# A phase-mixer layer with a ternary feed-forward: 16 token-sum blocks folded to 12 by an f16 add on VectorE

## The chip, the cores and the metric

The kernel runs on one core of one Trainium2 chip. The metric is device time in microseconds (us) of one execution; three runs of the kernel before gave 1516.4, 1513.59 and 1516.25 us, with a median of 1516.25 us.

## The reference

The input x has 16 sequences of 1024 tokens of 256 features. A first half normalises x over its features, and computes from it a phase and a memory:

```
omega = x @ W_omega.T + b_omega
phi   = cumsum(omega * exp(log_scale) / sqrt(position))          # over the sequence
cm_real, cm_imag   = x * cos(phi), x * sin(phi)
mem_real, mem_imag = cumsum(cm_real) / position, cumsum(cm_imag) / position
ret_real = mem_real * cos(phi) + mem_imag * sin(phi)
ret_imag = mem_imag * cos(phi) - mem_real * sin(phi)
context  = concat([cm_real, cm_imag, ret_real, ret_imag])         # 1024 features
h = gelu(layernorm(context) @ W1.T + b1) @ W2.T + b2              # 1024 -> 512 -> 256
x = x_input + x + h
```

The second half normalises again and adds `relu(x @ Wq1.T + b1) @ Wq2.T + b2`, 256 to 1024 to 256, with both weights rounded to -1, 0 or 1.

The layer norm of the context needs, for each token, the sum of its 1024 context features and the sum of their squares. The sum is what the change is about.

## The kernel before

The 16384 tokens are cut into 32 chunks of 512. Most tensors lie turned, with features on the 128 partitions and the 512 tokens of a chunk along the free dimension; so the 1024 context features are 8 blocks of 128x512 (`KC` = 8). Every f32 value that goes into a product is split into a high f16 half and a low f16 half (`ch` and `cl` for the context, made on ScalarE at line 645 and on VectorE at line 1382), and a product takes three passes: high by high, low by high, high by low.

The program is a pipeline written out by hand, one stream for each engine. Step s works on four chunks at once: `now` = s in the second half (the feed-forward), `nxt` = s+1 in the context's W1, gelu and W2, `ahead` = s+2 in phase, sums and retrieval, and `far` = s+3 in the first norm and omega. Steps run from -1 to 31. Within a step each engine's order is fixed by the program; engines meet by semaphores.

TensorE's order in a step is: `hidden` 0 and 1 (two of the four blocks of W1 on `nxt`, 24 matmuls each, line 989), `context_stats` (lines 959 and 965), `hidden` 2, `spread` (line 972, four transposes that spread the reciprocal deviation of each token over the partitions), `hidden` 3, then `ffn_in` 0 to 7 (line 1010) with `ffn_out` (line 1029) three blocks behind and `omega` (line 946) in between, `mixer_out` (W2, line 1060, 48 matmuls), and the last three `ffn_out`. `context_stats` gets the token sums by taking a 128x128 block of the context as the stationary operand and one column of ones as the moving one: for each of four token tiles, 16 such matmuls (8 blocks, high and low half) add into one PSUM column. Eight more do the same for the squares.

VectorE's order in a full step is: `fraction` (1300), `statistics_1` (1220 to 1230), `lean_2` (1236), `modulate_imag` (1313), `sums_imag` (a scan, 1321), `gains_1`, `modulate_real` (1307), `context_variance` (1387 to 1399, reads the token sums), `second_lo` (1442), `memory_imag`, `sums_real`, three `scale_hidden` (1406, which scale a finished `hidden` block and release its PSUM bank; `ffn_in` m waits for `scale_hidden` m), `first_rows_lo` (1264), `memory_real`, `retrieve_imag_cos`, the fourth `scale_hidden`, then the eight `relu_lo` (1450) among `gelu_lo` (1411), `context_lo` (1382) and others, `mixer_residual` (1418, waits for `mixer_out`), the phase scans (1287) and `statistics_2`.

GpSimd takes the power -1/2 three times (486, 510, 515), a product of 128x1024 into `qa` (563), additions of the squares (549, 556), and issues accumulating DMAs: `qa` is added into `rr` (491) and `qb` into `ri` (494). The sync engine's queue, in each step, waits for and issues four transposing loads of `turned2` (446), four of `turned1` (454), the load of the x rows four chunks on (458), and a store (461). In step -1 only some parts run; in step 0 VectorE also makes the signs of the second ternary weight (`signs(1)`, 1603 and 1604), and TensorE turns them.

In the last step `last_tiles` makes the output's last two blocks of products together, token tile by token tile, after VectorE's last `relu_lo`, and VectorE's `output` (1459) takes each half of the tiles as it is complete.

Of the kernel before, what the change touches and what calls it, by code (L numbers as in the profile page):

```python
# [17 lines left out]
ALU = mybir.AluOpType  # L18
# [25 lines left out]
def phase_mixer_layer(nc, x, w_omega, b_omega, log_scale, ln_gamma, ln_beta, w1, b1, w2, b2,  # L44
# [17 lines left out]
    with ctx:  # L62
# [98 lines left out]
        q_hi = sqr[:, 1, 0:CH // 2].bitcast(F16)  # L161
        q_lo = sqr[:, 1, CH // 2:CH].bitcast(F16)
        ones_h = sb("ones_h", [P, P], F16)
        turned2 = sb("turned2", [P, 2, KD, CH], F16)
        h2, l2 = turned2[:, 0], turned2[:, 1]
        rows1 = xs2[:, :, :].bitcast(F16).rearrange("p t (i d) -> p t i d", i=2)
# [123 lines left out]
        rl_done = sem("rl_done")  # L290
        f2_done = sem("f2_done")
        out_done = sem("out_done")
        tile_done = sem("tile_done")

        class Counts:

# [128 lines left out]
        def _(sp):  # L425
# [11 lines left out]
            sp.dma_start(pos_inv[:, :], pos_table[1].partition_broadcast(P)).then_inc(p_tab, 16)  # L437

            def step(s):
                if (c := s.chunk(0)) and c.index < CHUNKS - 1:  # L440
                    need(sp, h2_done, c)
                    need(sp, l2_done, c)
                    need_block(sp, f1_done, KF - 1, c, 1)
                    sp.sem_inc(turn2_begun, 1)
                    for j in range(NT):
                        sp.dma_start(turned2[:, :, :, j * P:(j + 1) * P].rearrange("p i k n -> p (i k) n"),
                                     rows2[:, j].rearrange("p i d -> p (i d)"), transpose=True).then_inc(turned2_done, 16)
                if (c := s.chunk(3)) and c.index >= 2:
                    need(sp, l1_done, c, 2)
                    need(sp, xf_done, c, 1)  # L450
                    need(sp, omega_done, c, 1)
                    sp.sem_inc(turn1_begun, 1)
                    for j in range(NT):
                        sp.dma_start(turned1[:, :, :, j * P:(j + 1) * P].rearrange("p i k n -> p (i k) n"),
                                     rows1[:, j].rearrange("p i d -> p (i d)"), transpose=True).then_inc(turned1_done, 16)
                if c := s.chunk(4):
                    need(sp, scaled_done, c, 2)
                    sp.dma_start(x_rows[:, c.b], x_v[c.index]).then_inc(x_loaded[c.b], 16)
                if (c := s.chunk(0)) and c.index < CHUNKS - 1:
                    need_dma(sp, x1_biased, c)  # L460
                    sp.dma_start(out_v[c.index], x1[:, c.b]).then_inc(stored[c.b], 16)
# [13 lines left out]
        def _(pool):  # L475
# [41 lines left out]
            def step(s):  # L517
                before, now, nxt, ahead, far = s.chunk(-1), s.chunk(0), s.chunk(1), s.chunk(2), s.chunk(3)
                if nxt and not now:
                    square_lo(nxt, ahead)  # L520
                if ahead:
                    base_bias(ahead)
                if now:
                    inverse_std_2(now)
                if before:
                    output_sum(before)
                if nxt and now:
                    square_lo(nxt, ahead)
                if far:
                    inverse_std_1(far)  # L530
                if now:
                    x1_bias(now)
                if nxt:
                    inverse_std_context(nxt)
                if ahead:
                    product_imag_sin(ahead)
                    retrieve(ahead)
                if ahead:
                    square_sums(ahead)
# [18 lines left out]
            def product_imag_sin(c):  # L558
                need(pool, mi_done, c)
                need(pool, sin_done, c)  # L560
                need(pool, sumr_done, c)
                need_sum(pool, rr_done, c, 1)
                pool.tensor_tensor(qa[:, :, :], mi[:, :, :], sn[:, :, :], ALU.mult).then_inc(qa_done, 1)  # L563

            first, second = first_chunks(pool)
# [359 lines left out]
        def _(pe):  # L925
# [24 lines left out]
            def context_stats(c, after):  # L950
# [2 lines left out]
                    need(pe, cl_done[part], c)  # L953
                if after:
                    need(pe, u_done, after)
                for j in range(NT):
                    halves = [(a, k) for k in range(KC) for a in (ch, cl)]
                    for i, (a, k) in enumerate(halves):
                        pe.matmul(ps[:, 3, j:j + 1], a[:, c.b, k, j * P:(j + 1) * P], ones_h[:, 0:1],  # L959
                                  start=(i == 0), stop=(i == len(halves) - 1))  # L960
                need(pe, qh_done, c)
                need(pe, ql_done, c)
# [68 lines left out]
                                     skip_group_check=True)  # L1031
                return last

            def last_tiles(c):

                for m in range(KF - 2, KF):
                    need_block(pe, rh_done, m, c)
                    need_block(pe, rl_done, m, c)
                for j in range(NT):
                    for m in range(KF - 2, KF):  # L1040
                        last = ffn_tile(m, j)
                    last.then_inc(tile_done, 1)

            def mixer_out(c, before):
                if before and c.index < CHUNKS - 1:
# [26 lines left out]
            def step(s):  # L1072
# [11 lines left out]
                if nxt:  # L1084
# [12 lines left out]
                    if not now:  # L1097
                        for n in SIGN_GROUPS[2:4]:
                            turn_signs(n)
                        mixer_out(nxt, now)  # L1100
                        omega(far)
                        return
                if now and not ahead:
                    for m in range(KF):
                        ffn_in(now, m, nxt)
                        if nxt and m == KE - 1:
                            mixer_out(nxt, now)
                        if m >= LAG:
                            ffn_out(now, m - LAG)
                    for m in range(KF - LAG, KF if nxt else KF - 2):  # L1110
                        ffn_out(now, m)
                        if nxt and m == KF - 3:
                            last_transposes(nxt)
                    if not nxt:
                        last_tiles(now)
                    return
                for m in range(KF):
                    if now:
# [7 lines left out]
                if now:  # L1126
                    for m in range(KF - LAG, KF):
                        ffn_out(now, m)

            def bank_free(n):  # L1130
                used = [i for i in range(n) if group_banks[i] == group_banks[n]]
# [71 lines left out]
        def _(dve):  # L1203
# [175 lines left out]
            def context_lo(c, part, src):  # L1379
# [2 lines left out]
                dve.tensor_tensor(cl[:, c.b, 2 * part:2 * part + 2], src, ch[:, c.b, 2 * part:2 * part + 2],  # L1382
                                  ALU.subtract).then_inc(cl_done[part], 1)

            def context_variance(c):
                need(dve, stats_done, c)
                dve.tensor_scalar(cmu[:, :], ps[:, 3, 0:NT], 1.0 / (RSTD_SCALE * C), None, ALU.mult).then_inc(cmu_done, 1)
# [65 lines left out]
            def output(c):  # L1453

                need_dma(dve, x1_biased, c)
                for half in range(2):
                    dve.wait_ge(tile_done, 2 * half + 2)
                    to = x1[:, c.b, 2 * half:2 * half + 2]
                    dve.scalar_tensor_tensor(out=to, in0=ps_rows_a[:, 2 * half:2 * half + 2], scalar=down[:, 4:5],
                                             in1=to, op0=ALU.mult, op1=ALU.add).then_inc(out_done, 1)  # L1460
# [1 line left out]
            def last_mixer(now, last):  # L1462

                lean_2(now)
                second_lo(now)
                context_variance(last)
                for m in range(KE):
                    scale_hidden(last, m)
# [13 lines left out]
            def step(s):  # L1482
# [15 lines left out]
                if nxt and not now:  # L1498
                    dve.wait_ge(p_fw1, 16)
                    signs(0, fw1_in, fw1_signs)  # L1500
                if now and now.index == 0:
                    dve.wait_ge(p_fw2, 16)
                    dve.wait_ge(p_tern, 2)
                    signs(1, fw2_in, fw2_signs)
                if ahead:
                    modulate_imag(ahead)
                    sums_imag(ahead)
                if far:
                    gains_1(far)
                if ahead:  # L1510
                    modulate_real(ahead)
                    carry_imag(ahead)
                if nxt:
                    context_variance(nxt)
                if now:
                    second_lo(now)
# [227 lines left out]
```

## Time and profile before

| | |
|---|---|
| median of three runs | 1516.25 us (1513.59 to 1516.4) |
| the profiled execution, its own time | 1516.13 us |
| its span, first to last instruction | 1514.3 us |
| mean granted TensorE clock | 0.991 |
| TensorE matmuls busy | 1465.8 us (97%) |
| VectorE busy | 1407.2 us (93%) |
| ScalarE busy | 1255.6 us (83%) |
| GpSimd busy | 558.7 us (37%) |

Busy time is the union of an engine's instructions. Two instructions of one engine overlap a little in it (the next starts before the last has drained), so what an instruction costs in a packed queue is the distance from its start to the next one's start. The span leaves 1.8 us of the profiled execution's time outside.

### The profile page before, as it was taken

To read this page: it belongs to the slowest core of one execution; us is meant where nothing else is said; L and a number is where in the kernel's file an instruction comes from. 1 tells how busy PE (TensorE), PEld (TensorE's weight loads), DVE (VectorE), ACT (ScalarE), POOL (GpSimd) and SP (SyncE) were. 2 spreads that over 40 slices of the span, in tenths; PEclk is the share of its full clock that TensorE was granted. 3 is DMA by queue.
4 is the path that set the end of the run, shared out by engine and by line. 5 is a ranking of instruction groups with operands and counts; after the bars stand their busy time and mean duration, and the time that the engine had idled before them with its cause. 6 is when DMAs were issued, how large, how long until landed. Compare 5 with 4: busy or idle time off the path is not lost.

```text
span 1514.3 us, 29961 instructions
## 1 busy us (share of the span) xinstructions
PE 1465.8 (97%) x10685; PEld 884.8 (58%) x10685; DVE 1407.2 (93%) x2325; ACT 1255.6 (83%) x1773; POOL 558.7 (37%) x393
## 2 busy tenths in 40 slices
PE   4789999999999999999999999999999999999998
PEld 2445566666566666555666655666655666665566
DVE  7989999999999999999999999999999999999844
ACT  6768888888888889888888888888888888888756
POOL 1223444333444433444433344443234443334321
PEclk9899999999999999999999999999999999999999
DMA  6436566656656666756666665666576566666542
GB/s 222 83 71 122 100 108 126 119 120 132 121 91 125 126 117 121 139 104 103 127 118 120 129 124 89 125 127 119 117 140 108 100 128 116 123 126 115 92 87 43
DMA packets 236035, 174.98 MB, mean 116 GB/s; under 512 B 139120, under 2 KB 222064, under 8 KB 235888
## 3 DMA queue, kind: packets, MB, share of 16 engines
q0 software_dynamic: 63984, 100.15, 40.5%
q1 hardware_dynamic: 170272, 69.25, 19.3%
q10 hardware_dynamic: 1632, 3.67, 0.7%
q8 instruction: 86, 1.41, 0.4%
q14 instruction: 61, 0.50, 0.1%
HBM read 24.13 MB, written 33.03 MB: 38 GB/s over the span
## 4 chain that ended last, share of the span: by engine, by line
PE 90%; DVE 4%; DMA 2%; issue 2%; ACT 2%; POOL 0%; ACTq 0%; DVEq 0%
PE ps L989 42%; PE ps L1029 14%; PE ps L1010 14%; PE ps L1060 11%; PE ps L946 5%; PE ps L959 3%; PE ps L972 1%; DMA arena<-in_L_attn_ln_beta 1%; DMA ri<-qb 1%; PE ps L965 0%; DVE mi L1321 0%; DMA rr<-qa 0%; DMA sqr<-turn 0%; ACT arena L716 0%; DVE bn L1220 0%
## 5 line engine op out<-in xcount | busy, mean ns | idle before, releaser
L989 PE MATMUL ps<-arena,w_hi 128*128 128x512 f16 x2048 | 610.3, 380 | 0.0
L989 PE MATMUL ps<-arena,w_lo 128*128 128x512 f16 x1024 | 388.7, 380 | 0.0
L989 PEld LDWEIGHTS ps<-arena,w_hi 128*128 128x128 f16 x2048 | 198.2, 98 | 221.3 <-issue 1.5
L1029 PE MATMUL ps<-fw_t,arena 128*128 128x256 f16 x2048 | 255.1, 273 | 3.0 <-DVE arena L1450 3.0
L1010 PE MATMUL ps<-turned,fw_t 128*128 128x512 f16 x1024 | 247.1, 379 | 0.4 <-issue 0.4
L1029 PEld LDWEIGHTS ps<-fw_t,arena 128*128 128x128 f16 x2048 | 199.9, 98 | 61.3 <-issue 13.7
L716 ACT ACTIVATE arena<-ps,relu_bias,relu_scale 128x512 f32<-128x512 f32 x256 | 196.8, 769 | 24.4 <-PE ps L1010 24.2
L1450 DVE TENSOR_TENSOR arena<-arena 128x512 f16<-128x512 f32 x256 | 173.1, 687 | 39.8 <-ACT arena L725 39.8
L1060 PE MATMUL ps<-w_hi,arena 128*128 128x256 f16 x1024 | 175.6, 275 | 4.8 <-DVE arena L1411 4.5
L989 PEld LDWEIGHTS ps<-arena,w_lo 128*128 128x128 f16 x1024 | 100.2, 98 | 121.3 <-issue 0.8
L725 ACT CAST arena<-arena 128x512 f16<-128x512 f32 x256 | 154.4, 614 | 4.3
L1010 PEld LDWEIGHTS ps<-turned,fw_t 128*128 128x128 f16 x1024 | 100.1, 98 | 93.7 <-issue 0.6
L1060 PE MATMUL ps<-w_lo,arena 128*128 128x256 f16 x512 | 140.9, 275 | 0.0
L491 POOL DMA_DIRECT2D rr<-qa x32 | 29.6, 925 | 226.1 <-DVE rr L1372 226.1
L549 POOL TENSOR_TENSOR sqr<-sqr 128x512 f32<-128x512 f32 x32 | 50.6, 1582 | 167.9 <-DVE arena L1382 153.8
L1060 PEld LDWEIGHTS ps<-w_hi,arena 128*128 128x128 f16 x1024 | 101.2, 99 | 17.9 <-issue 5.4
L563 POOL TENSOR_TENSOR qa<-mi,sn 128x1024 f32<-128x1024 f32 x31 | 73.2, 2361 | 86.4 <-DVE mr L1335 86.4
L613 ACT ACTIVATE xs<-x,lean,rs 128x256 f32<-128x256 f32 x128 | 66.4, 589 | 46.5 <-DVE lean L1236 46.5
L682 ACT ACTIVATE arena<-arena,b_full,z_down 128x512 f32<-128x512 f32 x128 | 96.9, 805 | 1.7 <-DVE arena L1406 1.3
L1406 DVE TENSOR_TENSOR arena<-ps,rb 128x512 f32<-128x512 f32 x128 | 82.1, 683 | 15.6 <-ACT rb L678 11.3
L1411 DVE SCALAR_TENSOR_TENSOR arena<-arena,up 128x512 f16<-128x512 f32 x128 | 95.0, 746 | 0.0
L546 POOL DMA_DIRECT2D sqr<-turn x32 | 27.4, 858 | 167.3 <-ACT turn L673 157.9
(189 smaller groups left out, 2805.2 us busy)
## 6 DMA issues: line engine op xcount, KB each, us to landing
x_rows<-in_L_attn_x SPq DMA_DIRECT2D x32, 512.0 KB, 4.6
rr<-qa POOLq DMA_DIRECT2D x32, 512.0 KB, 7.9
ri<-qb POOLq DMA_DIRECT2D x32, 512.0 KB, 8.5
sqr<-turn POOLq DMA_DIRECT2D x32, 512.0 KB, 5.5
base<-bias_rows POOLq DMA_DIRECT2D x32, 512.0 KB, 5.5
x<-bias_rows POOLq DMA_DIRECT2D x32, 512.0 KB, 5.9
out<-x SPq DMA_DIRECT2D x31, 512.0 KB, 5.7
out<-x POOLq DMA_DIRECT2D x31, 512.0 KB, 6.1
```

The lines of the kernel that those rows point to most:

```text
L563: pool.tensor_tensor(qa[:, :, :], mi[:, :, :], sn[:, :, :], ALU.mult).then_inc(qa_done, 1)
L682: act.activation(z[:, m], z[:, m], ACT.Gelu, scale=z_down[:, 0:1], bias=b1_full[:, m:m + 1])\
L716: act.activation(rf[:, m % SLOTS], ps[:, 4 + m % KE], ACT.Relu, scale=relu_scale[:, 0:1], bias=relu_bias[:, m:m + 1]).then_inc(relu_done, 1)
L725: act.copy(rh[:, m % SLOTS], rf[:, m % SLOTS]).then_inc(rh_done, 1)
L946: last = pe.matmul(ps[:, 2 + e], w[:, k, e * P:(e + 1) * P], a[:, k], start=(i == 0), stop=(i == len(passes) - 1))
L989: last = pe.matmul(ps[:, 4 + m], w[:, k, m * P:(m + 1) * P], a[:, c.b, k], start=(i == 0), stop=(i == len(passes) - 1))
L1010: last = pe.matmul(ps[:, 4 + m % KE], fw1_t[:, k, m * P:(m + 1) * P], a[:, k], start=(i == 0), stop=(i == len(passes) - 1))
L1029: last = pe.matmul(ps_rows_a[:, j], a[:, m % SLOTS, j * P:(j + 1) * P], fw2_t[:, m], start=(m == 0 and j % 2 == 0 and a is rh), stop=(m == ...
L1060: last = pe.matmul(rows[:, j], a[:, m, j * P:(j + 1) * P], w[:, m], start=(i == 0), stop=(i == len(passes) - 1))
L1406: dve.tensor_tensor(z[:, m], ps[:, 4 + m], rb[:, :], ALU.mult).then_inc(z_done[m], 1)
L1411: dve.scalar_tensor_tensor(out=gl[:, m], in0=z[:, m], scalar=up[:, 3:4], in1=gh[:, m], op0=ALU.mult, op1=ALU.subtract).then_inc(gl_done[m], 1)
L1450: dve.tensor_tensor(rl[:, m % SLOTS], rf[:, m % SLOTS], rh[:, m % SLOTS], ALU.subtract)\
```

## The change

VectorE gets a new instruction in each step, `fold_lo`: it adds the low halves of context blocks 4 to 7 to those of blocks 0 to 3, in f16, 128x2048 elements, into the buffer of `qa` (free at that time). TensorE's token sums then take the 8 high blocks and the 4 folded ones, 12 matmuls a token tile in place of 16, and wait for the fold; `qa`'s next writer on GpSimd waits for the sums. `fold_lo(nxt)` stands behind `modulate_imag(ahead)` in a normal step.

Besides: in step 0 `context_variance` stands ahead of `signs(1)`, and GpSimd's power for it ahead of a DMA issue; in step -1 TensorE does 12 products of 128x512 whose result nobody reads, ahead of `mixer_out`; the load of the x rows is first in the sync queue's step; and in the last step only the last block of products is held back, with the signal after each half of the tiles.

```diff
+        cl_fold = qa[:, :, :].rearrange("p k n -> p (k n)").bitcast(F16).rearrange("p (k n) -> p k n", k=KC // 2)
...
             def step(s):
+                if c := s.chunk(4):
+                    need(sp, scaled_done, c, 2)
+                    sp.dma_start(x_rows[:, c.b], x_v[c.index]).then_inc(x_loaded[c.b], 16)
                 if (c := s.chunk(0)) and c.index < CHUNKS - 1:
...
-                if c := s.chunk(4):
-                    need(sp, scaled_done, c, 2)
-                    sp.dma_start(x_rows[:, c.b], x_v[c.index]).then_inc(x_loaded[c.b], 16)
...
+                if nxt and now and now.index == 0:
+                    inverse_std_context(nxt)
                 if now:
                     x1_bias(now)
-                if nxt:
+                if nxt and not (now and now.index == 0):
                     inverse_std_context(nxt)
...
                 need_sum(pool, rr_done, c, 1)
+                need(pool, stats_done, c, 1)
                 pool.tensor_tensor(qa[:, :, :], mi[:, :, :], sn[:, :, :], ALU.mult).then_inc(qa_done, 1)
...
+                need(pe, clf_done, c)
                 for j in range(NT):
-                    halves = [(a, k) for k in range(KC) for a in (ch, cl)]
-                    for i, (a, k) in enumerate(halves):
-                        pe.matmul(ps[:, 3, j:j + 1], a[:, c.b, k, j * P:(j + 1) * P], ones_h[:, 0:1],
+                    halves = [ch[:, c.b, k] for k in range(KC)] + [cl_fold[:, k] for k in range(KC // 2)]
+                    for i, a in enumerate(halves):
+                        pe.matmul(ps[:, 3, j:j + 1], a[:, j * P:(j + 1) * P], ones_h[:, 0:1],
                                   start=(i == 0), stop=(i == len(halves) - 1))
...
-            def last_tiles(c):
-
-                for m in range(KF - 2, KF):
-                    need_block(pe, rh_done, m, c)
-                    need_block(pe, rl_done, m, c)
+            def last_unit(c):
+
+                need_block(pe, rh_done, KF - 1, c)
+                need_block(pe, rl_done, KF - 1, c)
                 for j in range(NT):
-                    for m in range(KF - 2, KF):
-                        last = ffn_tile(m, j)
-                    last.then_inc(tile_done, 1)
+                    last = ffn_tile(KF - 1, j)
+                    if j % 2:
+                        last.then_inc(pair_done, 1)
...
+                        need(pe, z_done[2], nxt)
+                        idle_products()
                         mixer_out(nxt, now)
...
+            def idle_products():
+
+                for i in range(12):
+                    pe.matmul(ps[:, 6], wo_hi[:, 0, 0:P], w1_hi[:, i % KC], start=True, stop=True)
...
+            def fold_lo(c):
+                need(dve, cl_done[3], c)
+                need_sum(dve, rr_done, c)
+                dve.tensor_tensor(cl_fold, cl[:, c.b, 0:KC // 2], cl[:, c.b, KC // 2:KC], ALU.add).then_inc(clf_done, 1)
...
+                if ahead:
+                    modulate_imag(ahead)
+                if nxt:
+                    fold_lo(nxt)
                 if now and now.index == 0:
+                    context_variance(nxt)
                     dve.wait_ge(p_fw2, 16)
                     dve.wait_ge(p_tern, 2)
                     signs(1, fw2_in, fw2_signs)
                 if ahead:
-                    modulate_imag(ahead)
                     sums_imag(ahead)
...
-                if nxt:
+                if nxt and not (now and now.index == 0):
                     context_variance(nxt)
```

## Rows read from the trace of the kernel before

**Rows 1.** The page: busy time, share of the span and instructions of the engines.

```profile
PE 1465.8 (97%) x10685; PEld 884.8 (58%) x10685; DVE 1407.2 (93%) x2325; ACT 1255.6 (83%) x1773; POOL 558.7 (37%) x393
```

**Rows 2.** The chain of waits in one middle step: start, us, what.

```profile
703.38 1.58 PE ps L959 x64
...
715.97 3.45 PE ps L1010 x16
...
735.08 2.62 PE ps L1029 x24
```

**Rows 3.** Busy times in that step; VectorE's largest wait over 16 steps.

```profile
693.01:737.70 44.69, 44.69 (x330) 26.91 (x328) 43.14 (x70) 38.38 (x55) 17.59 (x12) 1.00 0.63 119
...
DVE arena L1450 <- ACT arena L725: 12.7, 16, 0.9
```

**Rows 4.** Timeline of VectorE, then GpSimd, same step: start, us busy, instruction, [idle before].

```profile
699.03 1.58 DVE L1230 TENSOR_SCALAR ve<-mv 128x4 f32<-128x4 f32 x1
...
701.85 2.46 DVE L1321 TENSOR_TENSOR_SCAN mi<-ones,mi_carry,cmi 128x512 f32<-128x512 f32 x2
...
711.50 1.89 DVE L1406 TENSOR_TENSOR arena<-ps,rb 128x512 f32<-128x512 f32 x3 [0.30 <-ACT rb L678]
713.31 1.32 DVE L1264 TENSOR_TENSOR xs<-qb,xs 128x1024 f16<-128x1024 f32 x1
...
716.82 0.68 DVE L1406 TENSOR_TENSOR arena<-ps,rb 128x512 f32<-128x512 f32 x1
718.33 0.69 DVE L1450 TENSOR_TENSOR arena<-arena 128x512 f16<-128x512 f32 x1 [0.84 <-ACT arena L725]
...
734.47 0.68 DVE L1450 TENSOR_TENSOR arena<-arena 128x512 f16<-128x512 f32 x1
735.11 1.28 DVE L1418 SCALAR_TENSOR_TENSOR x<-ps,h_down,base 128x1024 f32<-128x1024 f32 x1
...
746.76 2.34 DVE L1321 TENSOR_TENSOR_SCAN mi<-ones,cmi 128x512 f32<-128x512 f32 x2
...
711.18 2.36 POOL L563 TENSOR_TENSOR qa<-mi,sn 128x1024 f32<-128x1024 f32 x1 [2.83 <-DVE mr L1335]
```

**Rows 5.** Groups of VectorE instructions nearest to the fold: count, busy us, mean ns.

```profile
L1313 DVE TENSOR_TENSOR cmi<-xf,sn 128x1024 f32<-128x1024 f32 x32 | 38.8, 1212 | 0.0
...
L1450 DVE TENSOR_TENSOR arena<-arena 128x512 f16<-128x512 f32 x256 | 173.1, 687 | 39.8 <-ACT arena L725 39.8
...
L1604 DVE TENSOR_SCALAR arena<-arena,neg_thr 128x2048 f16<-128x2048 f32 x1 | 1.3, 1275 | 0.0
```

**Rows 6.** Timelines, chain and one stretch of steps -1 and 0.

```profile
71.84 1.74 PE L959 MATMUL ps<-ones_h,arena 128*128 128x1 f16 x64
...
73.17 1.21 DVE L1313 TENSOR_TENSOR cmi<-xf,sn 128x1024 f32<-128x1024 f32 x1
...
82.55 1.88 DVE L1406 TENSOR_TENSOR arena<-ps,rb 128x512 f32<-128x512 f32 x3
...
91.43 0.58 SPq L458 DMA_DIRECT2D x_rows<-in_L_attn_x  x1
...
91.76 10.00 DMA ri<-qb
...
95.00:100.00 5.00, 5.00 (x27) 3.62 (x25) 3.48 (x3) 1.05 (x1) 0.00 (x0) 0.53 0.95 222
...
114.97 1.74 PE L959 MATMUL ps<-ones_h,arena 128*128 128x1 f16 x64
...
115.88 1.27 DVE L1603 TENSOR_SCALAR arena<-arena,thr 128x2048 f16<-128x2048 f32 x1
...
128.75 1.89 DVE L1406 TENSOR_TENSOR arena<-ps,rb 128x512 f32<-128x512 f32 x3
```

**Rows 7.** The chain of waits at the very end.

```profile
1508.78 0.14 issue
1508.91 1.92 PE ps L1029 x16
```

More of the change, by code:

```diff
@@ L292, in phase_mixer_layer @@
         out_done = sem("out_done")
-        tile_done = sem("tile_done")
+        pair_done = sem("pair_done")
+        clf_done = sem("clf_done")
         class Counts:
@@ L1109, in step @@
                             ffn_out(now, m - LAG)
-                    for m in range(KF - LAG, KF if nxt else KF - 2):
+                    for m in range(KF - LAG, KF if nxt else KF - 1):
                         ffn_out(now, m)
@@ L1114, in step @@
                     if not nxt:
-                        last_tiles(now)
+                        last_unit(now)
                     return
@@ L1456, in output @@
                 for half in range(2):
-                    dve.wait_ge(tile_done, 2 * half + 2)
+                    dve.wait_ge(pair_done, half + 1)
                     to = x1[:, c.b, 2 * half:2 * half + 2]
@@ L1465, in last_mixer @@
                 second_lo(now)
+                fold_lo(last)
                 context_variance(last)
```

## The prediction

> **What bounds the kernel now.** I read the page first. TensorE is busy for 97% of the span and VectorE for 93% [rows 1]. The chain of waits then shows that from about 140 to 1431 us it never leaves TensorE: every step has the same pieces, three of which stand in [rows 2], and no wait lies between them. The busy times by stretch give a step of 44.69 us with TensorE busy for all of it and VectorE for 43.14 [rows 3]; other steps give 44.67 to 44.69. So TensorE sets the step, with VectorE close behind. How close is the question, for the change takes work from the first and gives work to the second.
>
> VectorE's slack is read from its timeline [rows 4], between starts. Two of the 1406 instructions lie 0.60 apart ((1.89 - 0.68) / 2). The fourth starts at 716.82, so `relu_lo` 0 could start at 717.42; it starts at 718.33, behind ScalarE, which is itself behind TensorE's first `ffn_in`. That is 0.91 us of slack; over 16 steps the same wait is 12.7 us [rows 3], 0.79 a step as listed and 0.87 with the 0.07 by which packed instructions overlap. `mixer_residual` at 735.11 follows the `relu_lo` of 734.47 by 0.64, 0.04 over the packed distance: the end of `mixer_out` at 735.08 [rows 2] just holds it. The third wait, 0.30 us at 711.50, gives nothing back: the instruction behind those three, line 1264, takes 1.32 and only gets going when GpSimd's product ends at 711.18 + 2.36 = 713.54. An earlier start would only lengthen it. So a packed VectorE step is 44.68 - 0.87 - 0.04 = **43.77 us**. The small gaps between dependent tiny instructions stay.
>
> **What TensorE gives up.** 64 matmuls of one column take 1.58 us [rows 2], 24.7 ns each; 16 fewer give 0.39 us. Its own step becomes 44.29 us. If nothing else mattered, 28 such steps would gain 11 us.
>
> **What the fold costs.** No row shows a `tensor_tensor` with both inputs and output in f16. Its inputs are 2048 halves a partition, as many bytes as the 1024 f32 of line 1313, which takes 1.21 [rows 5] and, as 128x1024 instructions do, 1.14 from start to start. Line 1604 shows that VectorE can pass 2048 elements in 1.275 us, two for each it passes in the f32 instructions. If the fold went one element at a time, lines 1450 and 1313 extrapolate to 1212 + 2 x (1212 - 687) = 2262 ns, some 2.2 from start to start. Nothing points under 1.14. I take 1.14, the row with equal operation and equal bytes, and keep 2.2 as the far end.
>
> The Trainium skill ("VectorE: DVE Perf Modes", the perf-mode tier table) says that `tensor_tensor` on 16-bit data in SBUF runs at two elements a cycle, 1224 ns for 2048, and at one a cycle in fp32, 2293 ns. By the first the sum below stays as it is, by the second it is the third rival's. The table is about bf16, and no row here shows the f16 case.
>
> **The new step.** VectorE packed: 43.77 + 1.14 = 44.91 us, over TensorE's 44.29 and over the 44.68 of before. VectorE becomes the bound, and TensorE waits for it. Where it waits decides whether more is lost. Count from S, the start of `sums_imag` (701.85), right behind the fold. The fold ends at S + 0.08, and VectorE to TensorE takes 0.14 [rows 7], so the token sums start at S + 0.22 in place of S + 1.36 (703.21 on the timeline). With 0.39 less to do there, the first `ffn_in` comes 1.53 earlier relative to VectorE: at S + 12.43 (715.81 before; the chain sets the piece 0.16 later). `ffn_in` 3, 2.59 later, wants to go at S + 15.02. But it needs `scale_hidden` 3, which starts at S + 14.97 and ends at S + 15.65; with the hop it is free at S + 15.79. So TensorE stops there for 0.77 us. From there to the end of `mixer_out` TensorE needs what it needed before, 735.08 - 718.40 = 16.68, and ends at S + 32.47. VectorE would reach `mixer_residual`, packed, at 735.11 - 701.85 - 0.91 - 0.04 = S + 32.31, and starts at S + 32.50. That is 0.19 us more in each step, from a loop that runs fold, `scale_hidden` 3, `ffn_in`, `mixer_out`, `mixer_residual`. Then the rest of VectorE's step and the next fold follow unbroken. The step becomes 44.91 + 0.19 = **45.10 us, 0.42 more than before**. From step 0 to step 28, the last full one, that is 28 x 0.42 = **+11.8 us**; without the loop 28 x 0.23 = 6.4.
>
> Nothing else comes up in time by this count. `relu_lo` 0 needs 2.52 from the first `ffn_in`, S + 14.95, and VectorE is there at S + 15.57. GpSimd's power for the variance hangs on VectorE and is done 0.3 before `spread` asks. GpSimd's new wait for the sums ends at about S + 1.6, and its product starts at S + 9.3. The x rows are asked for 25 us sooner and leave the time in which `rr` and `ri` are added; nothing on the bound waits for those in a middle step, so this is worth nothing there. In the middle it could only matter by delaying the bias DMAs that it now meets, and those have most of a step.
>
> **The start.** In step -1 TensorE's sums stand at 71.84, but the fold comes behind line 1313 of 73.17 and ends near 75.5 [rows 6]. TensorE stops 3.8 us, `spread` comes some 3 us late, and line 1406 with it moves from 82.55 to about 85.2: +2.65 where the fold alone would be +1.14. That moves the issue of the `ri` addition from 91.76 to 94.4. It took 10.00 us, with the x rows issued at 91.43 in between; without them I take 8, so it lands at +0.6 (between -0.5 and +2.6). The 12 products fill about 2.6 us of TensorE's wait ahead of `mixer_out`, which before ran with the granted clock at 0.53 from 95 to 100 us, most of it at the lower level of 1.2 GHz. At the full clock that stretch would be 5.00 x 0.47 = 2.4 us shorter; that pays for the later start of `mixer_out` and no more. In step 0 the fold ends near 118.9 (115.88 + 0.6 + 1.14 + 1.22). TensorE's sums (114.97 before) wait 4 us for it, and then VectorE, with `context_variance` next in its queue, waits 1.6 for the sums. The four-odd instructions of the variance come sooner, but they only served a `spread` that isn't on VectorE's bound. VectorE reaches line 1406 near 132.1 in place of 128.75 and `relu_lo` 0 near 138.3. In the steady rhythm of before, counted back from 718.33 by 13 steps, it stood at 137.5. So the start costs **+0.8 to +1.0 us**, between -1 and +3.
>
> **The end.** In steps 29 and 30 VectorE has no `far` chunk and much idle time; the fold is hidden and TensorE gains 2 x 0.39. In the last step 8 of the 16 matmuls in the 1.92 us piece [rows 7] move ahead of VectorE's last `relu_lo`; VectorE's two 0.75 us instructions then follow one another, and 0.6 is gained. Together **-1.4 us**, with 0.1 given back where step 28 leaves TensorE.
>
> **Sum.** +11.8 + 1.0 - 1.3 = +11.5 on 1516.13 us of the profiled execution, whose time is 0.1 from the median: **1527.5 us**.
>
> **Rivals.** (1) VectorE bounds, but the loop through `scale_hidden` 3 doesn't close: 6.4 + 1.0 - 1.3, 1522 us. For it speaks that 0.19 hangs on a hop of 0.14 and two distances; against it that all of these are read from one regular step. With a good start 1519.5. (2) The other side: the fold finds room and TensorE stays the bound at 44.29: -11.0 + 1.0 - 1.3, 1505 us. That needs 0.62 us of VectorE's packed 44.91 to go. The one place is line 1230, a 128x4 instruction that takes 1.58 us [rows 4] and shares its time with one of GpSimd's additions; other 128x4 instructions of VectorE take 0.2. It decides if GpSimd's chain ends 0.62 us sooner relative to VectorE. Against it: that chain starts from VectorE's own line 1436, and nothing moves between them. (3) The fold runs one element at a time: 1.06 more in 28 steps and twice at the start, 1559 us.
>
> **Chances.** Forecast (1523 to 1531) 0.48; rival 1 (1517 to 1523) 0.27, of which a third falls below 1519.3; rival 2 0.13; rival 3 0.07; the rest, mixtures near no change, 0.05. The range that holds 8 in 10 leaves out rivals 2 and 3: 1516 to 1531. A measurement of this kernel tells 0.2%, 3 us, from no change. Faster 0.13, same 0.15, slower 0.72.
>
> **What would show it.** The step of the chain near 45.1 us; the fold at 1.2 us; no idle time before `relu_lo` 0 on VectorE; TensorE idle before line 1010 behind line 1406 (0.6 to 0.8 a step) and a little before line 959; 48 matmuls in 1.19. I am wrong if the step is 44.3 (then line 1230 is short), or if the fold takes over 2 us.

## The result

The changed kernel takes 1526.76 us (median of four runs, 1525.65 to 1527.73) against 1516.24 us before: a ratio of 1.0073 with a 95% interval of 1.006 to 1.0085. It is slower, as forecast, and 0.7 us from the forecast of 1527.5. Its profiled execution took 1527.73 us with a span of 1525.8, which is 11.5 above the span of before. The sum comes out right, but not all of its terms do. How they divide is the main subject below.

The page, the same line as [rows 1]. TensorE has lost 4.8 us of busy time and VectorE has gained 37.6. Below it stands the chain of waits by engine, in which VectorE now leads.

```profile
PE 1461.0 (96%) x10185; PEld 868.5 (57%) x10185; DVE 1444.8 (95%) x2357; ACT 1256.8 (82%) x1773; POOL 560.1 (37%) x393
...
DVE 40%; PE 33%; issue 13%; ACT 7%; DMA 3%; SPq 2%; DVEq 1%; POOL 0%; ACTq 0%
```

The groups by line, VectorE: the fold and the instructions around it (count, busy us, mean ns, idle before). Line numbers of after are some 5 to 17 higher: 1242 is the old 1230, 1276 the old 1264, 1423 is `scale_hidden`, 1435 `mixer_residual`, 1467 `relu_lo`, 951 `omega`, 965 the token sums, 995 `hidden`, 1016 `ffn_in`, 1035 `ffn_out`, 1065 `mixer_out`.

```profile
L1276 DVE TENSOR_TENSOR xs<-qb,xs 128x1024 f16<-128x1024 f32 x30 | 47.3, 1577 | 0.0
L1242 DVE TENSOR_SCALAR ve<-mv 128x4 f32<-128x4 f32 x32 | 44.8, 1401 | 1.2 <-DVE mv L1237 0.2
L1325 DVE TENSOR_TENSOR cmi<-xf,sn 128x1024 f32<-128x1024 f32 x32 | 40.8, 1275 | 0.1
L1400 DVE TENSOR_TENSOR qa<-arena 128x2048 f16<-128x2048 f16 x32 | 38.7, 1211 | 0.0
```

The busy times by stretch, one middle step, from one `mixer_residual` to the next; it answers to [rows 3]. TensorE now has gaps, and what VectorE lacks to the full stretch is some 0.5 us of small gaps between dependent tiny instructions.

```profile
743.95:788.82 44.87, 44.52 (x314) 26.35 (x313) 44.33 (x75) 38.26 (x54) 17.69 (x13) 1.00 0.63 118
```

The timeline of VectorE in that step: start, us busy, instruction. It answers to [rows 4].

```profile
743.30 0.68 DVE L1467 TENSOR_TENSOR arena<-arena 128x512 f16<-128x512 f32 x1
743.95 1.28 DVE L1435 SCALAR_TENSOR_TENSOR x<-ps,h_down,base 128x1024 f32<-128x1024 f32 x1
...
752.75 1.57 DVE L1242 TENSOR_SCALAR ve<-mv 128x4 f32<-128x4 f32 x1
...
754.30 1.21 DVE L1325 TENSOR_TENSOR cmi<-xf,sn 128x1024 f32<-128x1024 f32 x1
755.44 1.21 DVE L1400 TENSOR_TENSOR qa<-arena 128x2048 f16<-128x2048 f16 x1
756.58 2.33 DVE L1333 TENSOR_TENSOR_SCAN mi<-ones,cmi 128x512 f32<-128x512 f32 x2
...
771.36 0.68 DVE L1423 TENSOR_TENSOR arena<-ps,rb 128x512 f32<-128x512 f32 x1
771.96 0.68 DVE L1467 TENSOR_TENSOR arena<-arena 128x512 f16<-128x512 f32 x1
...
788.08 0.68 DVE L1467 TENSOR_TENSOR arena<-arena 128x512 f16<-128x512 f32 x1
788.82 1.28 DVE L1435 SCALAR_TENSOR_TENSOR x<-ps,h_down,base 128x1024 f32<-128x1024 f32 x1
```

The fold lies 1.14 from start to start, `relu_lo` 0 follows `scale_hidden` 3 at the packed distance of 0.60 with no idle time, and the last `relu_lo` stands 0.74 ahead of `mixer_residual` where 0.60 would be packed: 0.14 us of waiting for `mixer_out`. This step and the one of [rows 4] are not quite alike: every second step's scans carry on from the chunk before.

What TensorE waits for between 140 and 1420 us (total, times, longest):

```profile
PE ps L1016 <- DVE arena L1423: 8.3, 22, 0.6
PE ps L1016 <- DMA turned<-rows: 3.4, 5, 1.3
PE ps L951 <- DMA turned<-xs: 2.5, 1, 2.5
```

The first row is the stop that was forecast, `ffn_in` behind `scale_hidden` 3, seen 22 times, 0.4 us each as listed. The other two were not forecast: transposing loads that land late. The chain of waits of the same step shows the forecast loop closed, and its next piece behind the 5.25 us of `mixer_out` is VectorE again, by way of `mixer_residual`:

```profile
772.09 1.04 PE ps L1016 x4
...
783.54 5.25 PE ps L1065 x48
...
790.02 2.45 DVE ph L1299 x2
```

To see where the 11.5 us lie, take the start of `mixer_residual` in each step from VectorE's timeline (before: 154.50 in step 0 and 1405.31 in step 28; after: 157.16 and 1417.92). Up to step 0 the changed kernel loses 2.7 us, over the 28 steps 1260.76 - 1250.81 = 9.95, and from there to the end of the span it gains 1.1. Of the 28 steps most last 44.82 to 44.89, on average 44.85; a step of before lasts 44.68. So 28 x 0.17 = 4.8 us come from the regular step. Another 5.0 lie in a few long steps: 47.50, 45.77, 45.42 and smaller ones. The last 0.2 is the first of the 28, which before took only 44.46.

### The profile page after: what moved, and what is told of

Its sections match the earlier page's. It is cut to its first block, busy times and chain, and to the rows that moved or that the text cites. A ratio compares the mean times of both kernels' runs of the same rounds, so it can differ in the third digit from the quotient of the medians.

```text
span 1525.8 us, 29056 instructions
## 1 busy us (share of the span) xinstructions
PE 1461.0 (96%) x10185; PEld 868.5 (57%) x10185; DVE 1444.8 (95%) x2357; ACT 1256.8 (82%) x1773; POOL 560.1 (37%) x393
## 4 chain that ended last, share of the span: by engine, by line
DVE 40%; PE 33%; issue 13%; ACT 7%; DMA 3%; SPq 2%; DVEq 1%; POOL 0%; ACTq 0%
PE ps L1065 9%; PE ps L1016 8%; PE ps L1035 8%; DVE ph L1299 4%; PE ps L951 4%; DVE mr L1347 4%; ACT xs L618 3%; DVE arena L1423 3%; PE ps L995 3%; DVE bn L1232 3%; DVE mi L1333 3%; DVE bn L1442 3%; DVE xs L1276 2%; DVE cmr L1319 2%; DVE mi L1368 2%
## 5 line engine op out<-in xcount | busy, mean ns | idle before, releaser
L1016 PE MATMUL ps<-turned,fw_t 128*128 128x512 f16 x1024 | 251.3, 379 | 13.9 <-DVE arena L1423 8.3
L517 POOL TENSOR_TENSOR crs<-cve,minus_half 128x4 f32<-128x4 f32 x32 | 61.5, 1923 | 99.2 <-DVE cve L1416 99.2
```

The source lines that it names most:

```text
L1016: last = pe.matmul(ps[:, 4 + m % KE], fw1_t[:, k, m * P:(m + 1) * P], a[:, k], start=(i == 0), stop=(i == len(passes) - 1))
```

## The experiments

Theory A is the prediction's: VectorE is the bound, by the fold's time and a loop of 0.19. Rival B: the fold finds room in the stall of the old line 1230 and TensorE stays the bound. Times stand with the run of the kernel before on the same chip. "Step" is the regular distance between two `mixer_residual`, "start" its place in step 0. Unless said otherwise an edit is against the changed kernel.

### The fold and the sums without the other edits

The x loads, the order of step 0, the idle products and the last step are as before; the fold stands behind `modulate_imag`.

> The kernel before with the fold alone (fold, 12-block sums and their waits), none of the edits to the first steps, the last step and the order of the x load. Theory A (the time goes up because VectorE, packed, is longer than TensorE's step): a middle step near 44.9 us as in the changed kernel, so about 28 x 0.25 to 0.35 over before, plus some 4 us in steps -1 and 0, where nothing pays for the later sums: 1527 to 1530 us. Theory B (the other edits are what costs): close to 1505 us, 28 x 0.39 under before.

Measured 1535.95 us (1532.08 to 1539.16), ratio 1.0129 [1.0113, 1.0145]. The regular step is that of after, 44.84 to 44.87; the start is at 159.54. The four executions differ by 7 us. That is 6 us above the range expected of theory A, which held no long steps: 1266.37 - 28 x 44.85 = 10.6 us lie in them, where the changed kernel had 5.0. The regular steps account for 5, and the start for another 5. B is out.

### The other edits without the fold

```diff
-                need(pe, clf_done, c)
...
-                    halves = [ch[:, c.b, k] for k in range(KC)] + [cl_fold[:, k] for k in range(KC // 2)]
+                    halves = [(a, k) for k in range(KC) for a in (ch, cl)]
...
-                if nxt:
-                    fold_lo(nxt)
```

> The changed kernel without the fold: 16-block sums, all the other edits kept. Theory A: a middle step of 44.68 us as before, and some us less at the two ends: 1508 to 1514 us. Theory B: 1520 us or more.

Measured 1511.85 us (1511.27 to 1512.54), ratio 0.9971 [0.996, 0.9983]. They gain 3.4 us at the start (151.15 against 154.50) and 0.3 at the end; the step stays at 44.68. So the fold with its sums costs about 15 us in the changed kernel, and the rest gives back 4 of it.

### The fold ahead of the statistics

The stall of the old line 1230 is tested with the fold's place alone: ahead of `statistics_1(far)`, in place of behind `modulate_imag`.

```diff
+                if nxt:
+                    fold_lo(nxt)
                 if far:
                     statistics_1(far)
...
                 if ahead:
                     modulate_imag(ahead)
-                if nxt:
-                    fold_lo(nxt)
```

> The changed kernel with the fold moved ahead of the first-norm statistics of the far chunk in VectorE's order. There the 128x4 instruction that takes 1.56 us, because it meets GpSimd's addition, comes 1.14 us later and should meet only its last 0.4 us. Theory A1 (that stall ends with GpSimd's addition, whatever VectorE does before it): the fold fills the stall, VectorE packed comes to 43.8 us or less, TensorE is the bound again at 44.29 us, and the time is 1504 to 1508 us. Rival A2 (the stall has a length of its own and follows the instruction): the step stays near 44.9 us, the time at 1524 to 1527 us.

Measured 1505.35 us (1503.89 to 1505.8), ratio 0.9927 [0.9914, 0.9939]: the same instructions in another order are 21 us faster. Its timeline of VectorE, then of GpSimd:

```profile
738.42 1.22 DVE L1400 TENSOR_TENSOR qa<-arena 128x2048 f16<-128x2048 f16 x1
739.56 1.40 DVE L1232 BATCH_NORM_STATS2 bn<-x_rows 128x6 f32<-128x256 f32 x4
...
741.48 0.43 DVE L1242 TENSOR_SCALAR ve<-mv 128x4 f32<-128x4 f32 x1
...
740.22 1.66 POOL L560 TENSOR_TENSOR sqr<-sqr 128x512 f16<-128x512 f32 x1
```

And GpSimd in the changed kernel, beside line 1242 at 752.75 above:

```profile
752.62 1.66 POOL L560 TENSOR_TENSOR sqr<-sqr 128x512 f16<-128x512 f32 x1
```

GpSimd's addition ends at 754.28 in the one and at 741.88 in the other. Line 1242 ends at 754.32 and 741.91. So it ends when the addition does in both places, and most of its 1.57 us are a wait. The wait shrinks by 1.14, exactly the fold that now runs in it. GpSimd's chain hangs on a VectorE instruction ahead of the fold (line 1453), so the fold doesn't push it back: the addition starts 3.0 us after that instruction in both kernels. VectorE's step falls under TensorE's, and the step is 44.27 to 44.29 in 26 of 28 cases.

The Trainium skill ("SBUF — State Buffer", the section on SBUF's two separate sides) says that VectorE and GpSimd share one pair of ports, and that of a GpSimd instruction and a VectorE instruction that needs the pair (one in a mode that reads through two ports, or one with two inputs in SBUF) whichever starts first holds it for the whole instruction. The trace agrees in this place: GpSimd's addition starts first, 752.62 against 752.75 and 740.22 against 741.48, and both ends are 0.03 to 0.04 apart.

### Half the fold

Two blocks are folded, and 14 are summed.

```diff
-...+ [cl_fold[:, k] for k in range(KC // 2)]
+...+ [cl[:, c.b, k] for k in range(4)] + [cl_fold[:, k] for k in range(2)]
...
-dve.tensor_tensor(cl_fold, cl[:, c.b, 0:KC // 2], cl[:, c.b, KC // 2:KC], ALU.add)
+dve.tensor_tensor(cl_fold[:, 0:2], cl[:, c.b, 4:6], cl[:, c.b, 6:8], ALU.add)
```

> The changed kernel with half the fold: two low blocks are added to two others (128x1024 in f16), TensorE sums 14 blocks. Theory A: VectorE packed 44.85 - 0.53 = 44.32 us, TensorE 44.68 - 0.20 = 44.48 us and the bound again: 28 x 0.55 under the changed kernel, 1510 to 1513 us. Rival (TensorE loses its time by the wait for the fold as such, or by late transposing loads, and not by VectorE's length): a step between 44.7 and 45.0 us, 1519 to 1526 us.

Measured 1513.32 us (1511.75 to 1515.28), ratio 0.9981 [0.9973, 0.999]. The fold takes 678 ns, and most steps last 44.48: TensorE's 44.68 - 8 x 0.0247. VectorE, at 43.77 + 0.60, stays just below that, and the kernel isn't slower than before. The median is 0.3 above the range expected; the long steps (46.42, 45.25, 45.14 and smaller ones) hold 3.8 us in the profiled execution.

### The fold made and waited for, the sums over 16 blocks

```diff
-                    halves = [ch[:, c.b, k] for k in range(KC)] + [cl_fold[:, k] for k in range(KC // 2)]
+                    halves = [a[:, c.b, k] for k in range(KC) for a in (ch, cl)]
```

> The changed kernel with the fold made and waited for, but the sums over all 16 blocks as before. Theory A (VectorE, packed at 44.85 us, sets the step): giving TensorE its 0.39 us back costs nothing in the middle, since its 44.68 us are still the shorter; only the ends lose 0.8 us: 1523 to 1529 us, the lower half if waits for late transposing loads become rarer. Rival (TensorE's length still counts in full): 1538 us.

Measured 1534.11 us (1526.1 to 1536.17), ratio 1.0112 [1.0095, 1.013]. The regular step is 44.83 to 44.88, the same as after. The 16 matmuls saved are worth nothing in the changed kernel's regular step, since TensorE isn't its bound. The whole time doesn't show that: the median is 7 us over the changed kernel and 5 over the range expected, though still under the rival's 1538. In the profiled execution the start is 1.2 us later, the end 0.8 longer, and long steps hold 8.4 us in place of 5.0, one of them (51.20) 6.3. Why four of five executions take over 1533 us is not shown.

### Twelve blocks and no fold

This kernel leaves the low halves of the last four blocks out of the token sums.

```diff
-                    halves = [ch[:, c.b, k] for k in range(KC)] + [cl_fold[:, k] for k in range(KC // 2)]
+                    halves = [ch[:, c.b, k] for k in range(KC)] + [cl[:, c.b, k] for k in range(KC // 2)]
...
-                if nxt:
-                    fold_lo(nxt)
```

> The changed kernel without the fold and with 12 blocks summed all the same: the low halves of the last four context blocks are left out of the token sums. It prices the 16 matmuls alone. Theory A: a step of 44.29 us, 30 x 0.39 under the kernel without the fold, 1499 to 1501 us. Rival (matmuls of one column partly hide behind their neighbours): over 1504 us.

Measured 1502.48 us (1500.69 to 1503.97), ratio 0.9915 [0.9903, 0.9928], step 44.28. This is what the 16 matmuls are worth where VectorE pays nothing: 28 x 0.40. It confirms TensorE's side of the count in the step. The median is 1.5 us above the range expected; it is 9.4 under the kernel without the fold, where the two profiled spans differ by 11.8.

### The loop opened

`scale_hidden` 3 goes ahead of `retrieve_imag_cos` on VectorE, 1.14 us sooner.

```diff
-                    retrieve_imag_cos(ahead)
                 if nxt:
...
+                if ahead:
+                    retrieve_imag_cos(ahead)
```

> The changed kernel with the fourth scale_hidden one 128x1024 instruction earlier in VectorE's order (ahead of retrieve_imag_cos), 1.13 us sooner. TensorE's wait ahead of the fourth ffn_in, 0.6 us in most steps, should go, VectorE's work stays. If the loop through it costs the 0.19 us a step of the prediction: 28 x 0.19 less, 1521 to 1522 us. If VectorE's own length is nearly all of it (its wait ahead of mixer_residual is 0.05 to 0.14 in the trace): 1523 to 1526 us.

Measured 1522.41 us (1519.78 to 1530.02, six runs), ratio 1.0053 [1.0034, 1.0072]. The regular steps are 44.68 and 44.74, 44.71 on average, against 44.85. What TensorE waits for:

```profile
PE ps L951 <- DMA turned<-xs: 5.5, 2, 2.8
PE ps L1016 <- DMA turned<-rows: 4.4, 6, 1.6
```

The stop behind `scale_hidden` 3 is gone, and the distance from the last `relu_lo` to `mixer_residual` is 0.60 (787.71 to 788.31). The loop is real and costs 0.14 in each step; 44.71 is VectorE packed. The profiled execution itself had a span of 1528.0, with 10 us in long steps.

### The x load in its old place

```diff
-                if c := s.chunk(4):
-                    need(sp, scaled_done, c, 2)
-                    sp.dma_start(x_rows[:, c.b], x_v[c.index]).then_inc(x_loaded[c.b], 16)
                 if (c := s.chunk(0)) and c.index < CHUNKS - 1:
...
+                if c := s.chunk(4):
+                    need(sp, scaled_done, c, 2)
+                    sp.dma_start(x_rows[:, c.b], x_v[c.index]).then_inc(x_loaded[c.b], 16)
```

> The changed kernel with the load of the x rows back at its old place behind the transposing loads. In step -1 it meets the accumulating loads again: 1 to 2.5 us later. If it also is what made the middle 5.6 us longer in the kernel with the fold alone (steps in which TensorE waits for a transposing load): 1530 to 1534 us in all. If that was chance: 1527 to 1529 us.

Measured 1530.64 us (1526.35 to 1536.08), ratio 1.0097 [1.0081, 1.0113]. The start is at 161.60 in place of 157.16, 4.4 us later. With all the other edits undone as well (the first experiment) it was 2.4, so not all of this is the load's. One step lasts 51.28. Its chain of waits, and the stretches around it (the three figures at the end are the granted clock, the DMA share and GB/s):

```profile
1223.94 6.81 DMA turned<-xs
...
1230.80 5.30 PE ps L951 x12
```
```profile
1225.00:1230.00 5.00, 2.42 (x16) 1.27 (x13) 3.72 (x5) 4.93 (x9) 1.67 (x2) 0.98 0.92 139
1230.00:1235.00 5.00, 4.21 (x10) 1.49 (x11) 4.23 (x6) 2.06 (x3) 0.86 (x1) 0.50 1.07 289
```

The load lands after 6.81 us where 2.5 is the median. TensorE stops for 3.4 us, and the 12 `omega` matmuls behind it take 5.30 in place of 2.59, at a granted clock of 0.50, the lower level of 1.2 GHz. So this late load costs its 3.4 us and then 2.7 more at the lower clock. In the changed kernel the step of 47.50 is the same event with a stop of 2.5 us, and the granted clock stays at 1.00:

```profile
634.92 5.94 DMA turned<-xs
640.91 2.76 PE ps L951 x12
```

### Without the idle products

```diff
-                        need(pe, z_done[2], nxt)
-                        idle_products()
```

> The changed kernel without the 12 products in step -1 whose result nobody reads. By the prediction they spare mixer_out the lower clock, about 2.4 us, which only pays for its later start: if something waits for mixer_out in steps -1 and 0, 1528 to 1530 us. If the chain there runs through VectorE and the accumulating loads, no change: 1526 to 1528 us.

Measured 1529.06 us (1524.05 to 1530.29), ratio 1.0086 [1.0071, 1.01]. The stretch from 95 to 100 us, this kernel first, then the changed one:

```profile
95.00:100.00 5.00, 2.16 (x11) 1.53 (x12) 5.00 (x8) 3.57 (x5) 1.00 (x2) 0.50 0.97 184
```
```profile
95.00:100.00 5.00, 3.62 (x30) 2.64 (x29) 5.00 (x7) 3.39 (x4) 0.86 (x1) 1.00 1.07 201
```

The products keep the clock at its upper level, and step -1's `mixer_residual` starts at 105.00 in place of 105.89. By step 0 that is 0.6 us (157.16 and 157.78). The median lies in the range expected if something waits for `mixer_out`, but 0.6 us is too little for these medians to tell: long steps hold 7.1 us in this profile and 5.0 in the changed kernel's.

### The fold made twice

```diff
+                link(dve.tensor_tensor(cl_fold, cl[:, c.b, 0:KC // 2], cl[:, c.b, KC // 2:KC], ALU.add))
                 dve.tensor_tensor(cl_fold, cl[:, c.b, 0:KC // 2], cl[:, c.b, KC // 2:KC], ALU.add).then_inc(clf_done, 1)
```

> The changed kernel with the fold made twice, one behind the other, with a semaphore between them. Theory A (VectorE's packed length is the step): 1.14 us and a gap of 0.1 more in each of 28 steps and in both first steps, 1560 to 1566 us. Rival (part of the fold still lies in idle time of VectorE): under 1555 us.

Measured 1585.63 us (1582.34 to 1590.2), ratio 1.0475 [1.046, 1.0489], 20 us over what was expected. Part of the steps lasts 46.13 to 46.2, which is the changed kernel's 44.85 and some 1.3 more, as VectorE's time would have it. The others last 47.0 to 47.3. What TensorE waits for, and three stretches of one step:

```profile
PE ps L965 <- DVE qa L1401: 29.9, 27, 1.5
```
```profile
635.00:640.00 5.00, 4.05 (x33) 1.90 (x32) 4.96 (x6) 3.96 (x6) 4.18 (x3) 1.00 0.90 128
640.00:645.00 5.00, 5.00 (x58) 2.50 (x55) 4.93 (x13) 3.13 (x7) 1.08 (x1) 0.71 0.72 105
```

Behind each wait for the fold, TensorE does the small one-column products. In 19 of the 28 steps, those of 46.99 to 47.31, the granted clock then falls (0.71 over five us here, so part of it at the lower level, and 0.96 over the step); in the nine of 46.09 to 46.50 it is 1.00 throughout. So the second fold costs more than VectorE's time in it, and the rest is TensorE's clock. The length of the wait doesn't decide which steps fall: it was 0.9 to 1.3 us in the 19 and 1.2 to 1.5 in the nine. What does is open.

### The fold ahead of the statistics, and none for the first two chunks

The third experiment's kernel still started at 155.34, for in steps -1 and 0 nothing hides the fold. Here the first two chunks sum 16 blocks. The fold's move is the third experiment's and is left out of this cut.

```diff
-                need(pe, clf_done, c)
+                need(pe, clf_done, c, 2)
...
+                    low = [cl_fold[:, k] for k in range(KC // 2)] if c.index > 1 else [cl[:, c.b, k] for k in range(KC)]
...
             def fold_lo(c):
+                if c.index < 2:
+                    return
```

> The kernel with the early fold, with no fold for chunks 0 and 1, whose sums take 16 blocks. The middle stays at 44.28 us. In that kernel mixer_residual of step 0 starts at 155.3 us, in the one without the fold and with 12 blocks at 150.6. If the two folds and TensorE's waits for them are what fills those 4.7 us, up to 4 us come off 1505.35: 1500 to 1503 us. Rival (the start is set by other things there, the accumulating loads above all): 1504 to 1506 us.

Measured **1500.67 us** (1500.56 to 1500.84), ratio 0.9905 [0.9891, 0.9918]: 15 us faster than before, 26 faster than the change. One step, and the chain of waits in it:

```profile
740.00:784.28 44.28, 44.28 (x318) 26.52 (x316) 43.44 (x76) 38.38 (x55) 17.82 (x13) 1.00 0.64 120
```
```profile
738.94 1.18 PE ps L966 x48
...
765.00 5.24 PE ps L1066 x48
770.24 2.62 PE ps L1036 x24
772.86 7.34 PE ps L996 x34
```

TensorE is busy for all of it, as it was before the change, with a step shorter by the 0.40 of its matmuls. It even stands level with the kernel of twelve blocks and no fold (1502.48).

## Why the prediction came out, step by step

- **What bounds, and that it changes hands**: right. VectorE is the bound with a step of 44.85; that the 16 matmuls saved are then worth nothing is shown by the fold with 16 blocks (same step).
- **TensorE's 0.39 and its own step of 44.29**: right, 44.28 in three kernels.
- **The fold's 1.14**: right, 1211 ns busy and 1.13 to 1.14 from start to start. The far end of 2.2, and with it rival 3, is out.
- **VectorE packed, 44.91**: 0.20 too much; the loop-free kernel gives 44.71. This is the mis-sized term: 28 x (44.71 - 44.68) = 0.8 us, where 6.4 was forecast. I added the whole 1.14 to the packed step and said that the small gaps between dependent instructions stay. One does not. In [rows 4] the scan at 701.85 stands 1.25 behind the start of its producer `modulate_imag` (700.60), 0.11 more than the packed 1.14. With the fold between the two, the scan starts 1.14 + 1.14 = 2.28 behind it. So the fold costs 1.03 to 1.04. That explains half of the 0.20. The other half doesn't lie in the wait at 711.50, which I gave no value, rightly: from the start of line 1255 (711.04) to that of line 1349 (714.55) it was 3.51, and in the loop-free kernel's like step the same stretch is 3.50, for what the wait gives back line 1264 takes. It is spread over the step, in distances 0.01 to 0.02 shorter, and is unexplained.
- **The loop of 0.19**: right in kind, 0.14 in size, shown by opening it. The stop that was put at 0.77 is 0.51 in the step shown (772.09, where 768.99 + 2.59 = 771.58 was wanted). 28 x 0.14 = 3.9 us where 5.3 was forecast. Rival 1 is out.
- **Sum of the regular steps**: 4.8 us where 11.8 was forecast.
- **"Nothing else comes up in time by this count"**: this is the step that failed. The transposing loads come up in time. They hang on VectorE, and I had myself counted that the first `ffn_in` comes 1.53 earlier relative to VectorE, but not asked for the transfer between the two. The timelines of the sync engine's queue and of TensorE show it, before the change first:

```profile
707.54 5.38 SPq L446 DMA_TRANSPOSE turned<-rows  x4
715.81 3.62 PE L1010 MATMUL ps<-turned,fw_t 128*128 128x512 f16 x16
```
```profile
762.19 5.13 SPq L451 DMA_TRANSPOSE turned<-rows  x4
768.99 2.75 PE L1016 MATMUL ps<-turned,fw_t 128*128 128x512 f16 x12
```

  From the first issue to `ffn_in` there were 8.27 us (8.09 in the next step, whose scans are like those of the second line), and now there are 6.80. The fourth load is issued some 3.9 in and lands after 2.5 at the median, so 0.4 us is left where it was 1.7 to 1.9. Any landing over 2.9 now stops TensorE, which is what the five waits of up to 1.3 are. For `omega`'s loads the room shrank from 8.0 to 7.2. A stop of TensorE reaches VectorE by way of `mixer_out` and lengthens the step. The long steps add 5.0 us in the profiled execution. Only part of that is the lost room: a landing of 5.94 would have stopped TensorE before the change too, by 0.8 us less.
- **The start, +1.0**: +2.7, within the bounds of -1 to +3. The chain of waits there:

```profile
95.10 7.66 DMA ri<-qb
...
132.84 4.00 DMA turned<-rows
136.88 1.05 PE ps L1016 x4
```

  The addition of step -1 landed in 7.66 us (I took 8), but was issued at 95.10 and not at 94.4. In step 0 a load of `rows` came last, and not VectorE, whose queue alone I had followed: the same miss as in the middle. Without the fold the other edits give 151.15, so the fold costs 6.0 us at the start. Of the 2.4 us that the idle products were to give, 0.9 arrives at `mixer_residual` of step -1 and 0.6 at that of step 0.
- **The end, -1.3**: -1.1. Right.
- **Rival 2, the other side**: rightly rejected for the change as it is, and half right about the place. The stall of line 1230 was the one place where 0.62 us could go. I saw only one way, that GpSimd's chain ends sooner, and wrote that nothing moves between them. The other way is to put the fold into the stall. It gives 1505.35 us, and 1505 was the figure of that rival.

So the direction and the bound were right, but that the sum came within 1 us is luck, by errors of opposite sign: 7.0 us too much for the regular steps, and 5.0 (long steps), 1.7 (start), 0.2 (end) and 0.2 (the short first step of before) too little. The kernel with the fold alone showed it: its long steps, which no forecast held, take 10.6 us, and it came out 6 us past what was expected.

What stays open is why some transposing loads land in 5 to 7 us and most in 2.5, and how often in an execution. Before the change the longest between 140 and 1420 us was 4.1, and TensorE's matmuls waited for none. One execution of a kernel says little, but the profiles together say more. In the six in which TensorE sets the step (before, no fold, early fold, half fold, twelve blocks, the last kernel) the long steps hold 0 to 3.8 us; in the six in which VectorE sets it by one fold they hold 5.0 to 10.6, and the executions of one kernel lie 2 to 10 us apart, in place of 0.3 to 5.4. The kernel with two folds is the exception: TensorE waited 0.6 us in all for these loads. That the lost room is the cause, and that the late loads are what spreads the executions, is argued, not shown. Whether the place of the x load has a part in it is not settled: 5.0 us of long steps with it early, 8.9 with it late, from one profile each.

## What to carry to other kernels

An instruction that takes eight times what others of its size take is likely a wait, and a wait is a slot: look at what ends it on the other engine, and put new work of the same engine just ahead of it, behind whatever starts the other engine's chain. Here that decided between +10.5 and -10.4 us for the same instructions. When a change brings a consumer closer to its producer, look up every transfer that starts at the one and ends at the other, and compare the room left with its longest landing, not its median. And charge an insertion by the distance between the starts of its neighbours, as it may fill a gap that a dependence left.

## What was not expected of the hardware

- A 128x4 `tensor_scalar` on VectorE ended with GpSimd's 128x512 addition (within 0.04 us) and took 1.57 us so; started 1.1 later, it took 0.43.
- With the fold made twice, a wait of 0.9 to 1.5 us on TensorE and one-column products stood in each of 28 steps; in 19 of them the granted clock fell behind them (0.71 over 5 us in one), in nine it did not, and these had waits as long. A stop of 3.4 us was followed by 5 us at 0.50, one of 2.5 us by 5 us at 1.00.
- The transposing load for `omega`, with a median landing of 2.5 us, took up to 4.0 us before the change, 5.9 in the changed kernel, and 6.8 with the x load late.
